# A transformer block with two-choice experts in split float32 on one core: TensorE's expert tiles as a loop over groups of four slices, first-layer weights split per tile into a ring of four, the last tile's columns cut in steps of 32

## The reference, cut to what matters

```python
gates = softmax(x_flat @ gating_w); topk_w, topk_idx = top_k(gates, 2)      # 8 experts, 4096 tokens
valid = position < capacity                                              # capacity 1280 per expert
h = maximum(einsum('ecd,edh->ech', buf, w1) + b1[:, None, :], 0.0)        # 512 -> 2048
out_e = einsum('ech,ehd->ecd', h, w2) + b2[:, None, :]                     # 2048 -> 512
out = x + sum over the two choices of gathered * weight
```

## Time and profile before

| | us |
|---|---|
| median of 3 runs | 1946.61 |
| lowest, highest | 1945.52, 1947.61 |
| the profiled execution's own time | 1947.44 |
| span of its trace | 1945.8 |
| PE busy in it | 1924.3 |
| DVE, ACT, POOL busy in it | 1021.0, 631.0, 811.2 |
| TensorE clock granted, mean | 0.999 of full speed |

### The profile page before, as it was taken

How to read it: one execution, slowest core, us unless ns; L and a number is a source line. 1 busy time by engine, 2 the same in 40 slices (tenths; PEclk the granted TensorE clock), 3 DMA queues, 4 the chain that set the end, 5 groups by cost and what they waited for, 6 DMA issues and landing times.

```text
span 1945.8 us, 31039 instructions
## 1 busy us (share of the span) xinstructions
PE 1924.3 (99%) x10114; PEld 1699.2 (87%) x10115; DVE 1021.0 (52%) x1857; ACT 631.0 (32%) x977; POOL 811.2 (42%) x972
## 2 busy tenths in 40 slices
PE   8999999999999999999999999999999999999998
PEld 8899999998889899989988888889888888988897
DVE  5467787868534644455443623544436335445442
ACT  4434444445312432243222311322224223223221
POOL 2112336376754463445443332354443333523542
PEclk9999999999999999999999999999999999999999
DMA  6245555458122421252113403321044044133311
GB/s 170 99 120 153 162 168 142 131 142 238 39 46 60 145 53 30 41 152 66 28 34 108 107 16 86 102 69 26 16 132 108 18 108 108 43 79 108 70 28 26
DMA packets 150990, 174.06 MB, mean 89 GB/s; under 512 B 40366, under 2 KB 94766, under 8 KB 150928
## 3 DMA queue, kind: packets, MB, share of 16 engines
q1 hardware_dynamic: 120560, 134.16, 23.1%
q0 software_dynamic: 30368, 39.11, 11.3%
HBM read 124.33 MB, written 53.11 MB: 91 GB/s over the span
## 4 chain that ended last, share of the span: by engine, by line
PE 96%; DVE 1%; issue 1%; DMA 1%; ACT 0%; POOL 0%; POOLq 0%; SPq 0%; DVEq 0%
PE bank L1677 18%; PE bank L1680 18%; PE bank L1681 18%; PE pair_v L1677 8%; PE pair_v L1680 8%; PE pair_v L1681 8%; PE pair_o L1681 5%; PE pair_o L1677 5%; PE pair_o L1680 5%; PE bank L1860 1%; PE pair_v L1956 1%; PE pair_o L1956 1%; PE bank L1687 1%; DMA stage<-L_attn_v_w_dram 0%; PE pair_o L1860 0%
## 5 line engine op out<-in xcount | busy, mean ns | idle before, releaser
L1170 DVE CAST h_hi<-h 128x512 fp32r<-128x512 f32 x320 | 143.7, 449 | 727.6 <-ACT h L882 727.0
L675 POOL DMA_INDIRECT xg<-normed,quad_rows x304 | 312.7, 1029 | 380.4 <-PE pair_v L1681 294.4
L1677 PE MATMUL bank<-w_hi,h_hi 128*128 128x512 f32 x752 | 294.8, 392 | 2.1 <-DVE h_lo L1172 2.0
L1680 PE MATMUL bank<-w_lo,h_hi 128*128 128x512 f32 x752 | 295.1, 392 | 0.0
L1681 PE MATMUL bank<-w_hi,h_lo 128*128 128x512 f32 x752 | 294.7, 392 | 0.0
L882 ACT ACTIVATE h<-bank,b_cur 128x512 f32<-128x512 f32 x160 | 110.1, 688 | 536.0 <-PE bank L1681 535.7
L708 POOL DMA_INDIRECT out_dram<-ys,tab_s x80 | 132.5, 1657 | 360.0 <-DVE ys L1163 339.9
L882 ACT ACTIVATE h<-pair_v,b_cur 128x512 f32<-128x512 f32 x160 | 110.2, 689 | 446.2 <-PE pair_v L1681 446.1
L1677 PE MATMUL bank<-et_hi,w_hi 128*128 128x384 f32 (+2 forms) x640 | 226.3, 354 | 2.0 <-issue 1.4
L1172 DVE TENSOR_TENSOR h_lo<-h,h_hi 128x512 fp32r<-128x512 f32 x320 | 222.1, 694 | 11.0
L1681 PE MATMUL bank<-et_hi,w_lo 128*128 128x384 f32 (+2 forms) x640 | 226.0, 353 | 0.0
(11 more groups left out here) (292 smaller groups left out, 3723.5 us busy)
## 6 DMA issues: line engine op xcount, KB each, us to landing
w_raw<-L_ffn_w_dram SPq DMA_DIRECT2D x128, 512.0 KB, 4.0
xb<-_attn_hidden_states_dram SPq DMA_DIRECT2D x32, 256.0 KB, 3.3
xr<-_attn_hidden_states_dram SPq DMA_DIRECT2D x32, 256.0 KB, 3.6
out_dram<-x SPq DMA_DIRECT2D x32, 256.0 KB, 3.9
normed<-x1n SPq DMA_DIRECT2D x32, 256.0 KB, 3.8
x_quads<-xn SPq DMA_DIRECT2D x21, 256.0 KB, 2.6
xn<-x_quads SPq DMA_DIRECT2D x21, 256.0 KB, 4.0
a_quads<-at SPq DMA_DIRECT2D x21, 256.0 KB, 2.3
```

Of the source, the lines that this page charges most:

```text
L675: nc.gpsimd.indirect_dma_start(out=xg[:, h, P * a:P * (a + 1)], out_offset=None, in_=normed_quads, in_offset=bass.IndirectOffsetOnAxis(ap= ...
L1170: ve_.tensor_copy(h_hi[:, mm % 4, :], h32[:, mm % 2, :]).then_inc(h_split_hi, 1)
L1677: ins = mm_(out_, lh, rh, start=(first and c == 0), stop=False, skip_group_check=shared)
L1680: mm_(out_, lh, rl, start=False, stop=False, skip_group_check=shared)
```

## The change

**First-layer weights.** `w1_raw` keeps an expert's raw weights for all its tiles. For every tile anew, ACT and DVE split one slice of 128 hidden units (128x512 numbers) after each `relu` and `hidden`, four slices ahead, into a ring of four (`w1_hi`, `w1_lo`). SP loads the next expert's pieces when the last tile's split is through with them (`w1_ready` in place of `h_full`). A buffer `spare` fills the space that is left.

**PE's tile** is a loop `Fori(0, 4)` over `q`, with four slices `s = 4q + j` written out. The waits for the weights, for the bank and for S(n)'s input stand ahead of the branches; before the loop stands the wait on `et_ready`, with a `carry`. For each slice there are eight forms of F, of four or three blocks and four widths each, under nested branches. S(n) takes w2's slice by a register. The last `second_block` and `last_blocks` stand after the loop.

**The cut.** `width` is the count of tokens in the last block in steps of 32, less one. Only the last tile of an expert is cut, whichever size it has, by `32 * (3 - width)` columns, in all 16 slices. The plan has 11 DVE operations less, and the tables keep rows in the order of the tiles.

```diff
-        def threes_of(eng, e):
+        def width_of(eng, e):
 
             n = eng.value_load(plan[0:1, bass.ds(e, 1)], min_val=0, max_val=1024 * (TPE * E + 1) + 1023)
-            return (n >> 6) & 3, (n >> 8) & 3
+            return (n >> 6) & 3
...
-            raw("w1_raw", [P, KC, HID])
-            b("w1_lo", [P, KC, HID], F32R)
-            b("w1_hi", [P, KC, HID], F32R)
+            b("w1_raw", [P, KC, HID])
+            b("w1_hi", [P, RING, KC, P], F32R)
+            b("w1_lo", [P, RING, KC, P], F32R)
+            b("spare", [P, KC, HID // 2])
...
-        TRIMMED = 14
+        STEP = P // 4
...
-                        sp.wait_ge(h_full, MC * g + s + 1)
+                        sp.wait_ge(w1_ready, MC * g + s + 1)
                         carry(sp)
                         load_w1(e + 1, s // 2)
...
+            def w1_split(e, g, n):
+
+                if n >= MC:
+                    g, n = g + 1, n - MC
+                if n % 2 == 0:
+                    act.wait_ge(w1_landed[n // 2], 16 * e + 16)
+                if not (isinstance(g, int) and MC * g + n < RING):
+                    act.wait_ge(h_full, MC * g + n - RING + 1)
+                nc.scalar.activation(w1_hi[:, n % RING], w1_raw[:, :, P * n:P * (n + 1)], ACT.Copy).then_inc(w1_split_hi, 1)
...
-                    if split and mm in W1_AT:
-                        w1_split(e + 1, W1_AT[mm])
+                    if mm + RING < MC or not last:
+                        w1_split(e + 1 if split and mm + RING >= MC else e, g, mm + RING)
                     if split and mm in W2_AT:
                         w2_split(e + 1, W2_AT[mm])
...
+                for mm in range(RING):
+                    relu(g + 1, mm)
+                    w1_split(e + 1 if split else e, g + 1, mm + RING)
+                    if split and mm > 0:
+                        w2_split(e + 1, mm + 4)
...
+            def w1_lo_part(g, n):
+
+                if n >= MC:
+                    g, n = g + 1, n - MC
+                dve.wait_ge(w1_split_hi, MC * g + n + 1)
+                ve_.tensor_tensor(w1_lo[:, n % RING], w1_raw[:, :, P * n:P * (n + 1)], w1_hi[:, n % RING].bitcast(F32),
                                   ALU.subtract).then_inc(w1_ready, 1)
...
+                    if mm + RING < MC or not last:
+                        w1_lo_part(g, mm + RING)
...
-            whole, first, all_, short = (plan_f[:, c, 0:E] for c in (WHOLE, FIRST, ALL, SHORT))
+            width = plan_f[:, WIDTH, 0:E]
...
+            planning(ve_.tensor_scalar(half_i[:], half_i[:], 5, 3, ALU.logical_shift_right, ALU.bitwise_and))
+            planning(ve_.tensor_copy(width, half_i[:]))
...
+            planning(ve_.scalar_tensor_tensor(out=packed, in0=width, scalar=64.0, in1=packed, op0=ALU.mult, op1=ALU.add))
...
-            def first_layer(e, g, s, cols_, begun=None):
-
-                if s % 2 == 0:
-                    pe.wait_ge(w1_ready, PAIRS * e + s // 2 + 1)
+            def first_ready(g, s):
+
+                pe.wait_ge(w1_ready, MC * g + s + 1)
                 pe.wait_ge(h32_done, MC * g + s + 1)
+
+            def first_product(j, cols_):
+
+                product(h_bank[j % 2][:, 0:cols_], lambda k: (w1_hi[:, j, k, :], w1_lo[:, j, k, :]),
+                        lambda k: (et_hi[:, k, 0:cols_], et_lo[:, k, 0:cols_]), KC).then_inc(h_full, 1)
+
+            def first_layer(e, g, s, cols_):
+
+                first_ready(g, s)
                 if s == 0:
                     pe.wait_ge(et_ready, KC * g + KC + 1)
-                cols = slice(P * s, P * (s + 1))
-                product(h_bank[s % 2][:, 0:cols_], lambda k: (w1_hi[:, k, cols], w1_lo[:, k, cols]),
-                        lambda k: (et_hi[:, k, 0:cols_], et_lo[:, k, 0:cols_]), KC, begun=begun).then_inc(h_full, 1)
-
-            def hidden_ready(e, g, n):
-
-                if n % 2 == 0:
+                first_product(s % RING, cols_)
+
+            def hidden_ready(e, g, n, pair=None):
+
+                if pair is not None:
+                    pe.wait_ge(w2_ready, PAIRS * e + pair + 1)
+                elif isinstance(n, int) and n % 2 == 0:
                     pe.wait_ge(w2_ready, PAIRS * e + n // 2 + 1)
                 pe.wait_ge(h_ready, MC * g + n + 3)
-                if n == 0 and not (isinstance(g, int) and g == 0):
+
+            def output_free(g):
+
+                if not (isinstance(g, int) and g == 0):
                     pe.wait_ge(y_done, BT * (g + 1))
 
-            def block_product(n, h):
+            def second_weights(n):
+
+                at_ = nc.s_assert_within(n, 0, MC - 1, skip_runtime_bounds_check_because="n runs over the slices")
+                return tuple(w[:, bass.ds(at_, 1), :].rearrange("p a d -> p (a d)") for w in (w2_hi, w2_lo))
+
+            def block_product(n, h, slot=None, first=None):
 
                 toks = slice(P * h, P * (h + 1))
-                return product(y_bank[h][:], lambda k: (h_hi[:, n % 4, toks], h_lo[:, n % 4, toks]),
-                               lambda k: (w2_hi[:, n, :], w2_lo[:, n, :]), 1, first=(n == 0), last=(n == MC - 1))
+                slot = n % 4 if slot is None else slot
+                right = (w2_hi[:, n, :], w2_lo[:, n, :]) if isinstance(n, int) else n
+                return product(y_bank[h][:], lambda k: (h_hi[:, slot, toks], h_lo[:, slot, toks]), lambda k: right, 1,
+                               first=(n == 0) if first is None else first, last=isinstance(n, int) and n == MC - 1)
 
...
-            def tile(e, g, t, threes, whole, short):
-
-                for s in range(MC + LAG):
-                    with pe.If(t >= threes):
-                        if s < MC:
-                            first_layer(e, g, s, TT)
-                        if s >= LAG:
-                            fourth_block(e, g, s - LAG)
-                    if s < MC:
-                        idle = y_full if s == MC - 1 else None
-                        if s < TRIMMED:
-                            with pe.If(t < whole):
-                                first_layer(e, g, s, 3 * P)
-                            with pe.If(t == short):
-                                first_layer(e, g, s, 3 * P - P // 2)
+            def tile(e, g, t, threes, extra, width):
+
+                key = (extra - t) * 4 + width
+                pe.wait_ge(et_ready, KC * g + KC + 1)
+                carry(pe)
+                with pe.Fori(0, MC // RING) as q:
+                    for j in range(RING):
+                        s, n = q * RING + j, q * RING + j - LAG
+                        slot = (j - LAG) % 4
+                        first_ready(g, s)
+                        for blocks, test in ((4, t >= threes), (3, t < threes)):
+                            with pe.If(test):
+                                for narrow in range(4):
+                                    with pe.If(key == narrow if narrow < 3 else key >= 3):
+                                        first_product(j, P * blocks - STEP * (3 - narrow))
+                        if j < LAG:
+                            with pe.If(q >= 1):
+                                hidden_ready(e, g, n, q * 2 - 1 if j == 0 else None)
+                                carry(pe)
+                                n = second_weights(n)
+                                with pe.If(t >= threes):
+                                    block_product(n, Y_ORDER[0], slot, False)
+                                three_blocks(e, g, n, slot, False)
                         else:
-                            with pe.If(t < threes):
-                                first_layer(e, g, s, 3 * P, begun=idle)
-                    if LAG <= s < MC + LAG - BY_BLOCK:
-                        three_blocks(e, g, s - LAG)
-                    if s == MC - 1:
-                        second_block(e, g, MC - BY_BLOCK, MC - 1)
+                            hidden_ready(e, g, n, q * 2 if j == LAG else None)
+                            if j == LAG:
+                                output_free(g)
+                            carry(pe)
+                            n = second_weights(n)
+                            if j == LAG:
+                                with pe.If(q < 1):
+                                    with pe.If(t >= threes):
+                                        block_product(n, Y_ORDER[0], slot, True)
+                                    three_blocks(e, g, n, slot, True)
+                            with pe.If(q >= 1 if j == LAG else q >= 0):
+                                with pe.If(t >= threes):
+                                    block_product(n, Y_ORDER[0], slot, False)
+                                with pe.If(q < MC // RING - 1):
+                                    three_blocks(e, g, n, slot, False)
+                second_block(e, g, MC - BY_BLOCK, MC - 1)
+                with pe.If(t >= threes):
+                    fourth_block(e, g, MC - 2)
+                    fourth_block(e, g, MC - 1)
+                with pe.If(t < threes):
```

(3 more changed lines are left out.)

84 lines of the change are left out of this document (19 added, 65 removed).

## The result

The changed kernel takes 1981.18 us (median of four, 1976.32 to 1983.42) against 1947.11 for the kernel before beside it: slower, ratio 1.0167, interval 1.0141 to 1.0194. That is 34 us more, where 12 were forecast. The profiled execution is the fastest of the four: 1976.32 us, span 1974.7, which is 28.9 above the span before.

A forecast was written before the change was run, and what follows sets the result against it. PE's matmuls were taken to bound the kernel (PE busy 99%). Terms -16.6 + 15.5 + 6.2 + 7.2 = +12.3 on 1947.4, less 0.8, gave 1959 us; range 1935 to 1985.

The forecast's parts named there:

- in tile 0 the plan gets 11 operations shorter, beside matmuls: nothing: Tile 0: the plan's operations saved run beside matmuls, so they were costed at nothing.
- a register operand too dear to hide: S's matmuls with a register operand, in the 320-column tile: the case up to which the range's top, 1985, reached.
- The columns: First products of experts' last tiles: 3328 column-slices fewer, times 12 matmuls at 0.42 ns, -16.6 us.
- The starts after threes: Twelve tile starts after three-block tiles: first matmul late, 1.5 us for a whole three, +15.5 us together.
- The path of 2.4 us: PE's sequencer, from `et_ready` to a whole three's first matmul: carry, loop start, waits and branches, 2.4 us.
- The starts after fours: Tile starts after four-block tiles: 1.4 us more at three experts' starts, four others 0 to 0.95, +6.2 us.
- The third product: Third first product: the bank wait ahead of its branches leaves 0.55 us open in each of 13 threes, +7.2 us.
- 3.0 us of the sequencer's work in a slice: PE's sequencer, each slice: 3.0 us against 4.16 us of matmuls, hidden by the queue and costed at nothing.
- (1): Rival at `et_ready`: path to first matmul under about 1.2 us, starts stay covered; about -10, 1936 us; chance 0.22.
- Its weaker form: Rival (1) with every branch at the 0.13 us of one not taken: about -4, 1942 us.
- (2): Rival at S's nine register-operand matmuls: the sequencer bounds every slice; 62 us more, 2021, at 1.5 us a slice; chance 0.08.
- (3): Rival at PE's loop: code doesn't stay loaded, each of 57 jumps back fetches a block; +51, 2010 us; chance 0.04.

The follow-up runs named there:

- both: Changed kernel, w1 splits of slices 2 and 3 moved behind the next tile's rows, PE's first-product waits moved inside the width branches: 1959.7 us, ratio 1.0061.
- no_cut: Changed kernel with the width table set to full blocks, all branches kept: 2003.9 us.
- after_lean: Changed kernel without the second hidden_ready of each slice in tile 0 (6 PE instructions): 1976.5 us, ratio 1.0152.
- ring_alone: Kernel before with only the w1 ring's edits of ACT, DVE and SP, and PE's first-product waits and operands: 1959.4 us, ratio 1.0069.
- all_spread: all_in with the last six loads of expert 0 spread out, each behind one more slice of tile 0: 1945.5 us, ratio 1.0000.
- before_shift24: Kernel before with 24 semaphore instructions at the start of PE's program: 1945.5 us, ratio 0.9995.
- before_tail: Kernel before with 64 semaphore instructions behind PE's last loop: 1945.4 us, ratio 0.9996.
- all_in: Changed kernel with the edits of both, both_held, both_lean and after_order, and one load of the plan's word for two: 1944.9 us, ratio 1.0003.
- both_held: The kernel both, with SP holding the last five loads of expert 0's weights until PE has done five slices of tile 0: 1947.9 us, ratio 1.001.
- both_lean: The kernel both, without the second hidden_ready of each slice in tile 0: 1947.4 us, ratio 1.0008.
- late_splits: Changed kernel, ACT and DVE splitting the next tile's w1 slices 2 and 3 behind its rows, not ahead of them: 1963.8 us, ratio 1.0084.
- after_order: Changed kernel with the first product's branch tests reordered, three blocks before four and full width first: 1958.6 us, ratio 1.0074.
- both_shift128: The kernel both, with 128 semaphore instructions at the start of PE's program: 1961.1 us, ratio 1.0077.

## Why the prediction was wrong in size

**The step that failed** is "in tile 0 the plan gets 11 operations shorter, beside matmuls: nothing", and with it the silence on the rest of the static part. PE crawls there. The changed kernel without the crawl takes 1967.4 to 1967.8, with it 1981.2: 13 to 14 of the 34 us. That 1981 still lies below the 1985 of the range is luck: the range reached there for a register operand too dear to hide, and no slice between 4 and 14 of a three has a gap. What the runs show of it: it came in 11 of 16 kernels with the ring and in none of 4 without, always between 478 and 491 us, in five of them (both, no_cut, after_lean, ring_alone, all_spread) a second time between 506 and 520; PE stops inside products, and DVE stands 2 to 8 us between the same two operations in exactly those 11 kernels. The loads, PE's duplicate waits and PE's loop are not needed for it. It goes when 32 instructions are put ahead of DVE's program or of ACT's.

Three more facts stand in the traces. In exactly the 11 kernels the fourth raise of `cum_full` is on record 6 to 15 us behind PE's matmul, and 0.01 us behind it in the other five with the ring; so DVE stands since PE's count reaches it late, and not for want of its own code. The same 11 lose 437 to 589 records of semaphore raises each, the other five 0 to 3, and the loss begins at 290 us and goes on to the end; so the 32 instructions change something of the whole run, and not only of this stretch. And before_shift24 and before_tail lose as many records and don't crawl, so the loss alone doesn't make a crawl.

What delays the raises and holds PE inside its products stays open. One reading, which no run shows, is that code reaches PE and DVE too slowly when several engines' programs call for it at once. For DVE the raise at 484.81 speaks against that, and for PE all_in does, with no fetch on record from 480.1 to 495.7. A rival that no run tests is the recording itself: every execution here, the timed ones too, comes with a recorded span and clock, and where PE crawls records are lost. Why the hold of both_held or the 6 instructions of both_lean cured it in one kernel and not in another stays open as well. In the kernel before one packet of PE's code comes in as well, at 483.5 us, and PE is busy all the time from 480 to 490 us (10.00 of 10, 45 matmuls).

**The columns**, -16.6: right (3328 x 12 x 0.42 ns is 16.8 in full). By no_cut a column-slice is worth 26.1 / 5120 us, so 3328 are worth 17.0.

**The starts after threes**, +15.5: the sum is right, its place half. The 12 starts show 10.8 us more than before and slice 15 another 4.4, 15.2 in all. I had the product of slice 15 inside the same delay: PE waits there first, and what it waits is won back at the start. The path of 2.4 us from `et_ready` to a whole three measured 2.5 (the 2.2 above is of the three of 352 columns, with one branch taken less), `et_ready` came 1.2 us later by late_splits, and after_order shows that the branches are what is open.

**The starts after fours**, +6.2: 6.2 in the loops and 1.3 more at the first looped tile, which I had counted among the seven. An expert's start lies open for 2.0 us, 1.5 more than before, as forecast.

**The third product**, +7.2: 5.5; 0.42 us in each of 13 threes for 0.55.

**Left out of the sum**, in the loops, where 12.3 was forecast and 20.7 came: a gap of 0.1 to 0.45 ahead of F(1) (2.2 us), since its branches start only when F(0) has been handed on (in the tile above F(0) starts at 762.06, the sequencer's records ahead of F(1) run from 762.12 to 764.31, and F(1) starts at 764.36); 0.1 us that the first step behind each gap is longer, 0.27 for 0.174 (4.0 us over some 40 gaps); and two stretches at the clock of 0.50 behind an expert's start (about 3 us: in the tile at 1285 ten steps are 0.15 longer). With the terms above (-17.0 + 15.2 + 6.2 + 5.5) that gives 19.1 of the 20.7.

One sum of the forecast is off: its 3.0 us of the sequencer's work in a slice come to 2.8 (1.7, 1.0 and a quarter of 0.5). Nothing hangs on it, since I cost it at nothing there.

**The rivals.** (1) fell: `et_ready` to the first matmul is 2.2 to 2.5 us, and the gaps are there. Its weaker form, a branch taken at the price of one not taken, fell with after_order: a saving of 0.4 us a product would have been 8 us, and it was 15.6. The counts say the same in the kernel before: each of L1790 and L1792 is passed 266 times (19 tiles, 14 slices); L1790 is taken in the 8 tiles that aren't whole threes, 112 times, and its median is 77 ns; L1792 in the 17 that aren't cut, 238 times, and its median is 207. (2) fell: between F(3) and slice 14 no whole three has a gap. (3) fell as it stood: PE's last fetch is at 619 us, inside the first looped tile, and the 54 jumps back of the other 18 tiles come without one. The first pass through the loop's code isn't free, though. Its slowest branch takes 0.64 us in the changed kernel, 1.15 in both and 3.18 in all_in (at 565.2 us, while a packet of PE's code is under way), where later ones take 0.07 to 0.24. That PE could crawl where nothing branches was no rival of mine.

## What to carry to other kernels

In the changed kernel the six branches ahead of a first product cost nothing where the sequencer was ahead: no whole three has a gap between F(3) and slice 14. Behind a wait on the sequencer they lay open: waits moved behind them took 16.0 us from the loops, and the commonest case tested first took 15.6. So put the wait on the matmul, and test the commonest case first. These two, an order of work on DVE that serves the next wait first, and one load of the plan for two made the loops of this design 7 to 10 us shorter than the unrolled kernel's. And when a part that wasn't changed gets slower, look for gaps where the code has no wait, look when the semaphore that a standing engine waits for was raised, and shift one engine's program by a few instructions before you look for a cause in the work.

## What the hardware did that I had not expected

- PE slowed down in straight code, 22 matmuls in 10 us for 47, and its semaphore raises came late: 5 and 12 us at ACT there, 6 to 15 at DVE in the 11 kernels. In all_in PE did 9 matmuls in 5 us with the DMA queues idle (share 0.02). In the changed kernel 32 instructions at the start of DVE's or ACT's program cured it.
- The 128 semaphore instructions at the start of PE's program in both_shift128 started 0.15 us apart (1.3 to 20.7 us), and the kernel took 13 us more than both_held. Two loads of one word into a register started 0.7 us apart (1280.8 and 1281.5).
- The first step behind a gap was 0.1 us longer than the usual one: 0.27 us for 0.174 (762.06, 762.33, 762.50).
